# Two-layer block on eight cores: gram and scores from one product, q projected by tokens, ten evenly filled slots

## The reference, cut to what matters

```python
# layer norm, then this attention half, then a residual; then layer norm, an expert layer, a residual
q, k, v = proj(Wq), proj(Wk), proj(Wv)          # 16 heads of 64
k = k / max(norm(k), 1e-12)
def chunk_step(M, qkv):                          # chunks of 64 tokens, in sequence
    scores = where(mask, -inf, qi @ ki.T * scale)
    attn_out = softmax(scores) @ vi
    mem_out = qi @ M
    M, _ = scan(t_step, M, (ki, vi))             # M <- M - alpha (M k) k^T + beta v k^T, token by token
    return M, attn_out + 0.1 * mem_out
x = x + out @ Wo.T
```

## Time and profile before

| | us |
|---|---|
| median of 3 runs | 1457.8 |
| lowest and highest | 1455.4, 1459.3 |
| profiled execution | 1463.1 |
| its span, slowest core (core 0) | 1460.0 |
| its spans, all cores | 1445.7 to 1460.0 |
| TensorE busy of the span | 1176.9 (81%) |
| VectorE, ScalarE, GpSimd busy | 959.4, 814.2, 686.8 |

### The profile page before, as it was taken

The page is one execution under the profiler, slowest core; times in us unless marked ns, Lnnn a source line. Parts: engine busy times, 40 slices in busy tenths (PEclk is TensorE's granted clock), DMA queues, the critical chain, the costliest instruction groups (busy, mean ns, idle before and its releaser), DMA issues. The chain is left out here.

```text
span 1460.0 us, 72310 instructions; the slowest of 8 cores (1445.7 to 1460.0 us)
## 1 busy us (share of the span) xinstructions
PE 1176.9 (81%) x31168; PEld 768.4 (53%) x31168; DVE 959.4 (66%) x1325; ACT 814.2 (56%) x1187; POOL 686.8 (47%) x566
## 2 busy tenths in 40 slices
PE   1578888888888988888888888885577879777788
PEld 0355565555555555555555555553444466543665
DVE  2266776676767777667765666765667467873776
ACT  0155555555555555555555555563339866489775
POOL 3176666766667666676666766676201000011000
PEclk9789999999999999999999999996558789888999
DMA  9812222222222222222222222113124285741958
GB/s 155 145 39 43 45 46 53 47 43 45 46 53 47 45 47 46 52 46 49 45 45 45 50 43 42 27 30 74 30 73 152 77 273 157 235 153 42 279 144 241
DMA packets 75173, 122.35 MB, mean 84 GB/s; under 512 B 13408, under 2 KB 38000, under 8 KB 74864
## 3 DMA queue, kind: packets, MB, share of 16 engines
q1 hardware_dynamic: 48128, 92.30, 21.1%
q0 software_dynamic: 26736, 25.44, 13.2%
HBM read 117.93 MB, written 41.94 MB: 110 GB/s over the span
## 5 line engine op out<-in xcount | busy, mean ns | idle before, releaser
L807 DVE CAST W<-psW 128x1024 bf16<-128x1024 f32 x160 | 195.1, 1219 | 100.5 <-PE psW L602 98.5
L403 ACT CAST B<-psX 128x1024 bf16<-128x1024 f32 x128 | 129.8, 1014 | 87.4 <-PE psX L570 87.4
L803 DVE TENSOR_TENSOR AI<-A,eye 128x1024 bf16<-128x1024 bf16 x160 | 118.5, 757 | 44.2 <-ACT A L399 43.1
L1058 POOL TENSOR_TENSOR psel<-permT_sb,gmask_sb 128x256 bf16<-128x256 bf16 x32 | 19.8, 620 | 269.3 <-DVE permT_sb L1287 244.1
L519 PE MATMUL psD<-xnf,wq_sb 128*128 128x128 bf16 x2048 | 132.7, 224 | 14.3 <-DMA wq_sb<-wqT 7.9
L486 PE MATMUL psD<-wk_sb,xnf 128*128 128x512 bf16 x512 | 128.8, 397 | 18.3 <-DMA wk_sb<-wkT 13.1
L399 ACT CAST A<-psX 128x1024 bf16<-128x1024 f32 x128 | 130.2, 1017 | 19.0 <-PE psX L570 18.8
L495 PE MATMUL psD<-wv_sb,xnf 128*128 128x512 bf16 x512 | 128.8, 385 | 13.0 <-DMA wv_sb<-wvT 11.7
L545 PE MATMUL psD<-wo_sb,o_fm 128*128 128x512 bf16 x512 | 131.9, 393 | 1.3 <-issue 1.0
L519 PEld LDWEIGHTS psD<-xnf,wq_sb 128*128 128x128 bf16 x2048 | 120.5, 100 | 19.0 <-issue 16.2
L358 POOL TENSOR_TENSOR Ms_sb<-M_sb,b 128x1024 bf16<-128x1024 bf16 x31 | 68.7, 2215 | 128.8 <-DVE M_sb L851 128.8
(11 more groups left out here) (136 smaller groups left out, 2594.5 us busy)
## 6 DMA issues: line engine op xcount, KB each, us to landing
ring<-f1d SPq DMA_DIRECT2D x64, 256.0 KB, 4.0
ring<-f2d SPq DMA_DIRECT2D x64, 256.0 KB, 5.5
out<-ring SPq DMA_DIRECT2D x64, 256.0 KB, 4.0
xy<-x SPq DMA_DIRECT2D x68, 128.0 KB, 2.4
f1d<-f1w POOLq DMA_DIRECT2D x128, 64.0 KB, 2.5
f2d<-f2w POOLq DMA_DIRECT2D x128, 64.0 KB, 2.7
x1d<-x1b SPq DMA_DIRECT2D x64, 128.0 KB, 1.8
xy<-x1d SPq DMA_DIRECT2D x32, 256.0 KB, 3.1
```

The lines of the kernel that those rows point to most:

```text
L403: s.copy(B[k][:], psX[:, 0:1024]).then_inc(s_b, 1)
L803: v.tensor_tensor(heads(AI[k][:, :]), heads(A[k][:, :]), by_mask(eye2), ALU.add).then_inc(s_ai, 1)
L807: v.tensor_copy((Wf if k == 5 else W[k % 2])[:], psW[:, 0:1024]).then_inc(s_w, 1)
```

## The change

Four things, all in `phase_a`.

q is projected as k and v are: `q_part` with 16 matmuls of 512 columns, tokens by features, copied by ScalarE into q_tm, and then turned by eight transposes (`q_turn`) into psD1 read as bf16, from where VectorE copies it beside ka in one tile kaq.

The gram and the scores of tile j = i-1 are one group, `gram_and_scores`: 32 matmuls with k as the weights and [ka, q] as 128 columns, into psX and psY at once (psXY). ScalarE copies the gram half and then takes the exponential of the other half into one of two PT tiles. The scores of a tile are thus formed one pass earlier than before, GpSimd masks PT at the end of that pass, and the separate group of scores is gone.

The small groups are spread over ten slots: at most two groups of 32 behind each piece of projection, three in the last. Factors 0 to 3 of tile u come later in the pass, and factor 4 joins factor 5 in the next. k is turned in the seventh slot. A pass has 762 matmuls.

The orders of the other engines follow: the output copy opens the next pass on ScalarE, the sum of squares moves up on VectorE, k by its norm moves up on GpSimd. Waits are added for psX, psY (s_exp, s_lden) and for psD1 (s_qfm).

```diff
@@ -229,14 +230,14 @@
...
-q_fm = [sb(pa, f"qf{b}", [128, 1024]) for b in range(3)]
+q_tm = sb(pa, "q_tm", [128, 1024])
+kaq_fm = [sb(pa, f"kaq{b}", [128, 2048]) for b in range(3)]
...
-ka_fm = [sb(pa, f"ka{b}", [128, 1024]) for b in range(3)]
...
@@ -256,10 +257,15 @@
...
-psX = ps(pa, "psX", [128, 1024])
+psXY = ps(pa, "psXY", [128, 2048])
...
-psY = ps(pa, "psY", [128, 1024])
+psX, psY = psXY[:, 0:1024], psXY[:, 1024:2048]
...
+psT1 = psD1[:, :].bitcast(BF16)
+gram_scores = psXY[:, :].rearrange("p (h b c) -> p h b c", b=2, c=64)
+ka_fm = [kaq[:, 0:1024] for kaq in kaq_fm]
+q_fm = [kaq[:, 1024:2048] for kaq in kaq_fm]
...
@@ -353,35 +359,39 @@
...
+        if i < NT:
+            g.wait_ge(s_rk, 2 * i + 2)
+            g.tensor_tensor(heads(k_tm[i % 3][:, :]), heads(kraw[:, :]),
+                            rk[:, :].unsqueeze(2).broadcast_to([128, 16, 64]), ALU.mult).then_inc(s_ktm, 1)
+        cast(u, 2)
...
-        cast(u, 2)
-        if 0 <= u < NT:
-            g.wait_ge(s_exp, u + 1)
-            g.tensor_tensor(heads(PT[:, :]), heads(PT[:, :]), by_mask(mj), ALU.mult).then_inc(s_ptm, 1)
...
-        if i < NT:
-            g.wait_ge(s_rk, 2 * i + 2)
-            g.tensor_tensor(heads(k_tm[i % 3][:, :]), heads(kraw[:, :]),
-                            rk[:, :].unsqueeze(2).broadcast_to([128, 16, 64]), ALU.mult).then_inc(s_ktm, 1)
...
-        cast(u, 5)
...
-            g.tensor_tensor(Pn[:], PT[:], rden[:], ALU.mult).then_inc(s_pn, 1)
-        cast(u, 6)
+            if u > 0:
+                g.wait_ge(s_po, u)
+            g.tensor_tensor(Pn[:], PT[u % 2][:], rden[:], ALU.mult).then_inc(s_pn, 1)
+        cast(u, 5)
...
+            cast(u, 6)
+            g.wait_ge(s_exp, i)
+            g.tensor_tensor(heads(PT[(i - 1) % 2][:, :]), heads(PT[(i - 1) % 2][:, :]), by_mask(mj),
+                            ALU.mult).then_inc(s_ptm, 1)
+        else:
+            cast(u, 6)
...
-            g.tensor_tensor(ka_fm[i % 3][:, :].rearrange("p (a t) -> p a t", a=8),
+            g.tensor_tensor(ka_fm[i % 3].rearrange("p (a t) -> p a t", a=8),
...
@@ -412,14 +422,23 @@
...
-        s.copy(q_fm[i % 3][:, hf * 512:hf * 512 + 512], (psD0, psD1)[hf][:, :]).then_inc(s_q, 1)
+        if i > 0:
+            s.wait_ge(s_tq, i)
+        s.copy(q_tm[:, hf * 512:hf * 512 + 512], (psD0, psD1)[hf][:, :]).then_inc(s_q, 1)
...
+    def o_copy(e):
+        s.wait_ge(s_po, e + 1)
+        s.copy(o_fm[:, :].rearrange("p (a s c) -> p s a c", a=8, s=2),
+               psY.rearrange("p (s a c) -> p s a c", s=2, a=8)).then_inc(s_o, 1)
...
-        u = i - 2
+        u, e, j = i - 2, i - 3, i - 1
...
+        if 0 <= e < NT:
+            o_copy(e)
...
@@ -433,41 +452,39 @@
...
-        if proj:
-            v_half(i, 1)
-        if solve:
-            power_a(u, 3)
-            s.wait_ge(s_psc, u + 1)
-            s.activation(PT[:], psY[:, 0:1024], AF.Exp, scale=0.125).then_inc(s_exp, 1)
...
+            v_half(i, 1)
+        if solve:
+            power_a(u, 3)
+        if proj:
...
-        if i + 2 < NT:
-            ln_steps(i + 2)
+            s.wait_ge(s_pden, u + 1)
+            if u > 0:
+                s.wait_ge(s_pn, u)
+            s.activation(rden[:], psY, AF.Ln).then_inc(s_lden, 1)
...
+        if 0 <= j < NT:
+            s.wait_ge(s_pg, j + 1)
+            s.copy(heads(g_sb[:, :]), gram_scores[:, :, 0, :]).then_inc(s_g, 1)
+            s.activation(heads(PT[j % 2][:, :]), gram_scores[:, :, 1, :], AF.Exp, scale=0.125).then_inc(s_exp, 1)
...
-        if solve:
-            s.wait_ge(s_pden, u + 1)
-            s.activation(rden[:], psY[:, 0:1024], AF.Ln).then_inc(s_lden, 1)
-        if 0 <= i - 1 < NT:
-            s.wait_ge(s_pg, i)
-            s.copy(g_sb[:], psX[:, 0:1024]).then_inc(s_g, 1)
...
+        if i + 2 < NT:
+            ln_steps(i + 2)
+        if solve:
...
-            s.wait_ge(s_po, u + 1)
-            s.copy(o_fm[:, :].rearrange("p (a s c) -> p s a c", a=8, s=2),
-                   psY[:, 0:1024].rearrange("p (s a c) -> p s a c", s=2, a=8)).then_inc(s_o, 1)
...
@@ -477,9 +494,11 @@
...
+            if i > 3:
+                t.wait_ge(s_x1, 2 * (i - 3) - 1)
...
-                t.wait_ge(s_q, 2 * i)
+                t.wait_ge(s_qfm, i)
...
@@ -507,39 +526,41 @@
...
-    def q_half(i, hf):
+    def q_part(i, hf, lo, hi):
...
-        for oc in range(4 * hf, 4 * hf + 4):
-            for kc in range(8):
-                ins = t.matmul((psD0, psD1)[hf][:, (oc % 4) * 128:(oc % 4) * 128 + 128],
-                               wq_sb[:, kc * 1024 + oc * 128:kc * 1024 + oc * 128 + 128],
-                               xn_fm[i % 2][:, kc * 128:(kc + 1) * 128],
-                               start=(kc == 0), stop=(kc == 7))
-        ins.then_inc(s_pq, 1)
+        for kc in range(lo, hi):
+            ins = t.matmul((psD0, psD1)[hf][:, :], xn_fm[i % 2][:, kc * 128:(kc + 1) * 128],
+                           wq_sb[:, kc * 1024 + hf * 512:kc * 1024 + hf * 512 + 512],
+                           start=(kc == 0), stop=(kc == 7))
+        if hi == 8:
+            ins.then_inc(s_pq, 1)
...
-        if i > 2:
-            t.wait_ge(s_x1, 2 * (i - 3) + 1)
...
+    def q_turn(i):
+        t.wait_ge(s_q, 2 * i + 2)
+        for oc in range(8):
+            ins = t.transpose(psT1[:, oc * 128:(oc + 1) * 128], q_tm[:, oc * 128:(oc + 1) * 128], ident_bf[:])
+        ins.then_inc(s_tq, 1)
...
-            if e + 3 < NT:
-                t.wait_ge(s_q, 2 * (e + 3) + hf + 1)
-            else:
-                t.wait_ge(s_kfm, NT)
+            t.wait_ge((s_kfm, s_qfm)[hf], min(e + 4, NT))
+            if e + 3 >= NT:
...
@@ -548,16 +569,19 @@
...
-    def gram(j):
+    def gram_and_scores(j):
...
+        t.wait_ge(s_qfm, j + 1)
...
+            t.wait_ge(s_lden, j)
...
-                ins = t.matmul(psX[s * 64:s * 64 + 64, hr * 64:hr * 64 + 64],
-                               ka_fm[j % 3][r:r + 64, c:c + 64], k_fm[j % 3][r:r + 64, c:c + 64],
+                ins = t.matmul(psXY[s * 64:s * 64 + 64, hr * 128:hr * 128 + 128], k_fm[j % 3][r:r + 64, c:c + 64],
+                               kaq_fm[j % 3][:, :].rearrange("p (b x) -> p b x", b=2)[r:r + 64, :, c:c + 64],
...
@@ -582,6 +606,7 @@
...
+            t.wait_ge(s_exp, u + 2)
...
@@ -642,22 +667,11 @@
...
-    def scores(u):
...
-        ins.then_inc(s_psc, 1)
...
+        t.wait_ge(s_rhs, u + 1)
...
+            ins = t.matmul(psY[:, hf * 512:hf * 512 + 512], onesblk[:], PT[u % 2][:, hf * 512:hf * 512 + 512],
...
@@ -671,6 +685,8 @@
...
+        if u + 1 < NT:
+            t.wait_ge(s_exp, u + 2)
...
@@ -705,76 +721,79 @@
...
+        if proj:
+            q_part(i, 1, 0, 4)
+            k_turn(i)
         if 0 <= i - 1 < NT:
-            gram(i - 1)
+            gram_and_scores(i - 1)
+        if solve:
+            factor(u, 1)
+        if proj:
+            q_part(i, 1, 4, 8)
         if i == 3:
             t.wait_ge(s_wo, 16)
         if ends:
-            wo_part(e, 0, 0, 8)
+            wo_part(e, 0, 0, 4)
         if solve:
             power_a(u, 4)
+            factor(u, 2)
+        if proj:
+            q_turn(i)
         if ends:
-            wo_part(e, 1, 0, 4)
-        if proj:
-            k_turn(i)
...
@@ -832,45 +851,49 @@
...
+            v.wait_ge(s_pa, 5 * e + 5)
+            v.tensor_tensor(heads(AI[5][:, :])[:, :, 0:32], heads(psX)[:, :, 0:32],
+                            eye2[:, 0:32].unsqueeze(1).broadcast_to([128, 16, 32]), ALU.add).then_inc(s_ai, 1)
+            factor(e, 3)
+            factor(e, 4)
+        if solve:
+            plus_eye(u, 0)
+        if ends:
...
```

122 lines of the change are left out of this document (52 added, 70 removed).

## The result

The changed kernel takes 1513.8 us (median; 1513.4 to 1530.9) beside 1455.4 us (1452.8 to 1459.3) for the kernel before on the same chip: a ratio of 1.040, 95% interval [1.038, 1.042]. One of the five executions, the one of 1530.9, had the cores of one die at a lower clock and is left out of the ratio. The forecast was 1406, 3.6% faster.

The account below looks back on a forecast made before the run. It took TensorE, pausing for instruction blocks, as the bound. The pass falls by 1.7 us, -49 over 29 passes, -3 at the start: 1463.1 becomes 1411, less 5.3 for the median, 1406; 8 in 10 for 1362 to 1458.

Parts of the forecast that it names:

- the blocks: TensorE's instructions arrive in blocks of about 123 matmuls; it pauses when the next is late; 6.75 blocks a pass become 6.17.
- the sum: Sliding window of 123 matmuls over TensorE's pass: pauses where work falls short of the block interval, 4.0 us before.
- the last sum: Changed pass with waits included: 26.1 + 1.95 = 28.05 us, 1.65 under the 29.7 of before.
- T: Assumed constant interval between arriving instruction blocks on TensorE, taken as 4.1 us.
- Rival B: Each block crossing costs a pause whatever the spacing, so spreading wins nothing: likeliest 1458 us; chance 0.11.
- D: Even order lifts TensorE's instruction pauses wholly: -3.6 us a pass, 1350 to 1377 us; chance 0.12.
- The small waits: TensorE's new waits for other engines: 1.6 us a pass together, of which 70%, 1.1, counted.
- The bound on kss: VectorE's bound on the sum of squares, between H and M: taken as 0.2 us in its new place.
- E: Long bound (1.6 us) in the chain from H to M, waits of 3.1: 1437 to 1455 us; chance 0.06.
- The start: At the kernel's start, k's waits for copies of turned k go, against the turned q: -3 us.
- rival C: GpSimd holds VectorE's fourth plus_eye, possibly through PT's mask and ka: +1.0 us a pass, 1484 us; chance 0.12.
- the walk for the fourth B: ScalarE's chain from the gram's end to A: 5.2 us against TensorE's 4.5, so 0.7 wait, the largest.

Follow-up runs that it names:

- e8: Changed kernel with the fourth plus_eye reading the product from PSUM and the copy of turned q ahead of the normalisation: 1395.1 us, 0.961 of before.
- e6: Kernel before with v in 64 matmuls of 128 columns instead of 16 of 512: 1488.2 us, 1.025 of before.
- e12: e8 with q in 64 matmuls of 128 columns instead of 16 of 512: 1418.7 us, 0.973 of before.
- e2: Changed kernel with VectorE's copy of turned q ahead of the normalisation and the third factor's copy: 1561.1 us, 1.074 of before.
- e17: Changed kernel with GpSimd's two DMA issues of the casts placed between PT's mask and ka: 1545.5 us, 1.058 of before.
- e15: Changed kernel with eight wide unused matmuls in TensorE's wait before Wo's second half: 1532.2 us, 1.045 of before.
- e3: Changed kernel with VectorE's fourth plus_eye moved from the end of the pass into the next pass: 1456.1 us, 1.004 of before.
- e11: Changed kernel with the fourth plus_eye reading the product from PSUM as the one edit: 1452.2 us, 0.995 of before.
- e1: Changed kernel with ScalarE's two layer norm steps (rstd) back before the logarithm of the row sums: 1560.7 us, 1.077 of before.
- e16: e11 with six wide unused matmuls in the wait before Wo's second half: 1444.8 us, 0.986 of before.
- e18: e3 with eight wide unused matmuls in the wait before Wo's second half: 1449.9 us, 0.989 of before.

## Why the prediction was wrong, point by point

**What bounds the kernel, and the blocks: right in direction, the sizes partly by luck.** e8, the changed order with its two faults taken out, has passes of 28.7 us. The forecast was 28.05, times 30.5/29.7 for the profile's own passes 28.8. Its 1395 us are 0.8% from the 1406 on record. Pauses fell from 2.9 us a pass to 1.1 (median of the six cores with full records), and to 0.7 in the changed kernel; the sum had them fall from 4.0 to 1.95. Its work was too small, 24.5 us where TensorE is busy for 26.1 of each pass, and the two errors nearly cancel. And 26.1 in the last sum is not 24.7 + 1.1 = 25.8; no row gives the other 0.3. T explains e6 to within a few us, and doesn't explain e12. Rival B, which saw no gain in fewer blocks, is out by e6 and e8; D, no pauses at all, by e8's passes and its 1.1 us of pauses.

**The small waits: right.** Per pass, from the groups above: fourth B on ScalarE's A 0.4 (forecast 0.7, by the section on what would show it 0.5), `k_by_h` on M 0.3 (0.3), the gram on the row sums' logarithm 0.1 (0.2), the first half of q on the turned x 0.1 (0.2). The bound on kss took 174 ns (0.2), so E is out. The start gained 3.7 (3).

**The step that failed** is the sentence "VectorE gets one more copy, 0.68, but is busy for only 66% of the span: nothing, as long as that copy is done before the second half of Wo, 2.5 us of TensorE's work after the turn". It puts VectorE's part at nothing, names the condition and doesn't walk it, and the forecast left the hold of `plus_eye` to rival C. In its place the profile has 4.0 us a pass of waits for VectorE: 2.4 for the copy of q, 0.8 for the fifth AI and 0.7 for a factor's copy behind the held `plus_eye`. The copy ended 4.5 us after the turn. What delays it could have been found: the diff moves `rstd` behind rden's exponential on ScalarE, the walk for the fourth B even sums that chain (it put the two steps of layer norm in it), and the normalisation on VectorE, which waits for them, stands ahead of the copy. That walk asked only for what ScalarE's queue does to A, not who else waits for what is in it. A share of 66% says nothing of one stretch.

**Rival C was the mechanism, at 0.12 and with too low a price.** Rows 8 and 9 had shown the hold; the text itself named PT's mask and ka behind B and asked whether VectorE is passed over there too. It is, in every pass, 5.0 us. C priced that at 3.0 us of wait, a pass 1.0 longer than before, 1484. Measured was a pass 2.3 longer over the loop. C alone, on the forecast's own queue, never ran; e2, the nearest, is at 1.074, far over 1484. C's sum left out the late copy of q, and the clock, which in e2 slows what comes behind the hold. The chance was too low because the one release that rows 8 and 9 show, behind B, was taken for the rule, and because the two waits ahead of PT's mask and ka were held to be openings: both are already satisfied there, and e17 shows that even a microsecond without an operation is none.

**What the text didn't have at all** is the clock. It took 1.0 for granted since the kernel before runs at it for most of the loop. With a wait of some 2.4 us in each pass, the changed kernel is at half clock for 4.2 us a pass in the mean. Filling the wait for q's copy gains nothing there (e15); in e3 and e11 it gains 22 and 13 us. The Trainium skill, "TensorE: Matmul & The Clock Gate", section "HAM oscillation — how this bites in real kernels", has this pattern, a stall in each tile that leaves the engine cold for the next one; the windows of the changed kernel show it, about once a pass.

**How it adds up.** The forecast pass, 28.8, is what e8 measured, 28.7, so the changed kernel can be set beside e8, by the six cores of each with full records, from 400 to 700 us, in us a pass: waits for other engines 5.0 against 1.6, +3.4; TensorE busy 27.2 against 26.0, +1.2, its slower matmuls at half clock; pauses 0.7 against 1.1, -0.4. That is +4.2, where the passes of the two differ by 4.1. By intervention: `plus_eye` out of the hold -65 us (e11), the copy of q ahead of the normalisation then -49 (e8), the latter with the clock in it.

## What to carry to other kernels

An added instruction on a half-idle engine is priced by its place in that engine's queue: walk what stands ahead of it, what that waits for, and what was moved on the engine it waits for. Where two engines can hold each other up, look at which operation will meet which after the change; as long as a hold ends with the other engine's run, being earlier in front of it gains nothing, and one operand read from PSUM took it away. Cutting the pass at the end of the hold shows on which side of it a loss lies. When TensorE gets a new wait of a few microseconds in each pass, read the granted clock behind it, and ask whether the slow stretch falls behind a longer wait or into the path that sets the pass.

## What the runs showed of the hardware that I had not expected

- GpSimd's hold on a VectorE operation with two SBUF operands spanned up to three GpSimd operations and the DMA issues between them, 7.42 us for one of 0.68 (e1), and a gap of 1.03 us between two GpSimd operations did not end it (e17). In all cases read here the held operation ended 0.54 to 0.57 us behind the end of a GpSimd operation.
- The same add with one operand in PSUM took 1224 ns in the mean of eleven beside the same GpSimd work, and was not held (e8).
- TensorE's granted clock fell to half about once in each pass of the changed kernel, whose longest wait is some 2.4 us a pass, and stayed there for 4.2 us in the mean; filling the wait with unused matmuls made two kernels faster by 13 and 22 us (e16, e18).
- 48 more matmuls and weight loads a pass over the same columns cost 1.1 us a pass in the kernel before (e6), 0.4 in e8 (e12).
